# A mixture-of-experts and attention kernel whose scatters add into rows of x in DRAM

## What is computed

```python
x = x + 0.5 * ffn(layernorm(x), router, gate_up, gate_up_bias, down, down_bias)
x = x + attention(layernorm(x), Wq, bq, Wk, bk, Wv, bv, Wo, bo)
x = x + 0.5 * ffn(layernorm(x), ...)      # the same weights again
```

## Time and profile before

| | us |
|---|---|
| time, median of 3 runs | 704.48 (702.71 to 705.45) |
| the profiled execution: span, from first to last instruction | 799.3 |
| what lies around the span in the profiled execution | not shown |
| mean granted TensorE clock, as a share of full speed | 0.913 |

### The profile page before, as it was taken

How to read it: one execution, slowest core, us unless ns; L and a number is a source line. 1 busy time by engine, 2 the same in 40 slices (tenths; PEclk the granted TensorE clock), 3 DMA queues, 4 the chain that set the end, 5 groups by cost and what they waited for, 6 DMA issues and landing times.

```text
span 799.3 us, 13210 instructions
## 1 busy us (share of the span) xinstructions
PE 631.0 (79%) x3712; PEld 527.1 (66%) x3713; DVE 446.0 (56%) x1116; ACT 314.2 (39%) x696; POOL 353.5 (44%) x379
## 2 busy tenths in 40 slices
PE   2673898888878879969998996679898898888900
PEld 2452777776757668858887994568777786767700
DVE  6868653444434436277775986845353444445446
ACT  2663243434333335346663443334243334333400
POOL 2781646565656553513331000155656565656400
PEclk9985999999999998999999999599988999999955
DMA  9871232222222221245542431132212222222179
GB/s 307 295 229 28 73 99 81 70 78 69 85 72 78 78 73 52 93 135 157 157 142 94 150 116 66 8 87 67 79 62 85 70 82 69 79 72 79 54 261 369
DMA packets 52601, 87.99 MB, mean 110 GB/s; under 512 B 16228, under 2 KB 32019, under 8 KB 52054
## 3 DMA queue, kind: packets, MB, share of 16 engines
q1 hardware_dynamic: 17568, 39.52, 15.0%
q0 software_dynamic: 13664, 35.42, 14.3%
q10 hardware_dynamic: 21334, 12.61, 5.1%
HBM read 53.94 MB, written 35.39 MB: 112 GB/s over the span
## 4 chain that ended last, share of the span: by engine, by line
PE 61%; DVE 13%; another core or an unknown queue 8%; DMA 7%; issue 5%; ACT 4%; POOL 0%; SPq 0%; ACTq 0%; DVEq 0%; POOLq 0%
PE ps L854 15%; PE ps L852 13%; PE ps L853 12%; PE ps L843 9%; PE ps L1070 3%; DMA work<-y_dram 3%; PE ps L847 3%; DVE aT_lo L1447 2%; PE ps L877 2%; ACT aT_hi L689 2%; DVE xs L1503 1%; DMA raw_c<-L_ffn_down_proj 1%; PE ps L926 1%; PE ps L869 1%
## 5 line engine op out<-in xcount | busy, mean ns | idle before, releaser
L521 POOL DMA_INDIRECT y_dram<-work,sidx x142 | 142.7, 1005 | 166.7 <-ACT work L706 128.7
L513 POOL DMA_INDIRECT work<-xn_dram,gidx x142 | 140.2, 988 | 47.2 <-issue 43.6
L1455 DVE TENSOR_SCALAR work<-ps 128x256 f32<-128x256 f32 x142 | 57.1, 418 | 147.3 <-issue 83.3
L843 PE MATMUL ps<-cst,work 128*128 128x128 f32 x688 | 109.4, 284 | 29.9 <-DVE aT_lo L1447 22.5
L852 PE MATMUL ps<-up_hi,xT_hi 128*128 x284 | 120.9, 426 | 13.5 <-issue 11.2
L854 PE MATMUL ps<-up_hi,xT_lo 128*128 x284 | 114.1, 402 | 8.6 <-issue 8.2
L853 PE MATMUL ps<-up_lo,xT_hi 128*128 x284 | 113.8, 401 | 8.5 <-issue 7.8
L696 ACT ACTIVATE work<-ps 128x256 f32<-128x256 f32 x142 | 52.1, 393 | 171.7 <-PE ps L854 129.8
L843 PEld LDWEIGHTS ps<-cst,work 128*128 128x128 f32 x688 | 84.3, 145 | 52.3 <-issue 35.3
L852 PE MATMUL ps<-dn_hi,aT_hi 128*128 x284 | 96.7, 340 | 0.0
L706 ACT ACTIVATE work<-ps,slot_gate 128x256 f32<-128x256 f32 x142 | 59.5, 471 | 72.2 <-PE ps L854 54.7
(11 more groups left out here) (172 smaller groups left out, 1136.5 us busy)
## 6 DMA issues: line engine op xcount, KB each, us to landing
work<-y_dram SPq DMA_DIRECT2D x32, 512.0 KB, 4.3
xn_dram<-work ACTq DMA_DIRECT2D x29, 255.0 KB, 2.6
xs<-L_attn_x SPq DMA_DIRECT2D x4, 1024.0 KB, 10.5
work<-q_dram SPq DMA_DIRECT2D x16, 256.0 KB, 2.8
out<-xs SPq DMA_DIRECT2D x16, 256.0 KB, 5.9
q_dram<-work ACTq DMA_DIRECT2D x15, 256.0 KB, 2.3
work<-xn_dram,gidx POOLq DMA_INDIRECT x142
y_dram<-work,sidx POOLq DMA_INDIRECT x142
```

The costliest lines, as they stand in the source:

```text
L513: pool.indirect_dma_start(xg[:, k, u, 1:H + 1], None, xn_dram[n], bass.IndirectOffsetOnAxis(ap=gidx[:, 2 * s + u:2 * s + u + 1], axis=0)). ...
L521: pool.indirect_dma_start(y_dram[n], bass.IndirectOffsetOnAxis(ap=sidx[:, 2 * s + u:2 * s + u + 1], axis=0), ysb[:, k, u, :], None, bounds ...
L843: ins = nc.tensor.transpose(ps[:, bank, k:k + P], src[:, u, c * P:(c + 1) * P], ident)
L1455: return v.tensor_scalar(upv[:, u, :], ps[:, 2 + 2 * b + u, :].rearrange("p (f c) -> p f c", c=2)[:, :, 1], 1.0 - LIMIT, 1.0 + LIMIT, ALU. ...
```

## The change

- `y_dram` goes. In its place stands `sums_dram`, one row for each token and 128 spare ones. In layer 0 SP copies x into it, DRAM to DRAM, in four parts, behind the expert weights. In layer 1 SP stores each pair of xs to it once attention has been added (`x_done`).
- A scatter now adds its 128 rows to the rows of their tokens (`compute_op=ALU.add`). The two choices of a token come in different tiles. Each scatter waits until the one before it has landed; the first of a layer waits for the copy or the stores. The index `sidx` is the token's, or 4096 plus the partition for a slot without a token, and the bounds check is gone (three more VectorE operations in `route`, and SKIP's place).
- In GpSimd's step, gathers and scatters alternate: gather, scatter, gather, scatter.
- After layer 0 SP loads the sums straight into xs, 256 KB a pair, four in flight, each waiting only for the load four before it; `ybuf` and `combine` go.
- The end of layer 1 is four copies, DRAM to DRAM, of 1 MB each, from the sums to the output; the loads, additions and stores there go.

```diff
-        y_dram = [scratch(f"y_dram{n}", [T * TOPK, H]) for n in range(2)]
+        sums_dram = [scratch(f"sums_dram{n}", [T + P, H]) for n in range(2)]
...
+        def part(rows, q):
+
+            n = T // OUT_PARTS
+            return rows[q * n:(q + 1) * n, :].rearrange("(p i) h -> p (i h)", p=P)
...
             for e in range(2, E):
                 load_raw(e)
+            for q in range(OUT_PARTS):
+                sp.dma_start(part(sums_dram[0], q), part(x_rows, q)).then_inc(L[0].sums_begun, 16)
...
             wait_scattered(0)
-            for b in range(2):
-                sp.dma_start(ybuf[:, b], pair(y_v[0], b)).then_inc(L[0].y_loaded[b], 16)
+            for j in range(4):
+                sp.dma_start(pair(xs, j), pair(sums_v[0], j)).then_inc(L[0].sums_loaded[j], 16)
...
-            with sp.Fori(0, NG // 2 - 1) as it:
-                for b in range(2):
-                    g = it * 2 + b
-                    sp.wait_ge(L[0].y_used, g + 1)
-                    sp.dma_start(ybuf[:, b], pair(y_v[0], g + 2)).then_inc(L[0].y_loaded[b], 16)
-
-
-            sp.wait_ge(L[0].y_used, NG)
+            with sp.Fori(0, NG // 4 - 1) as it:
+                for j in range(4):
+                    sp.wait_ge(L[0].sums_loaded[j], 16 * (it + 1))
+                    sp.dma_start(pair(xs, it * 4 + (j + 4)), pair(sums_v[0], it * 4 + (j + 4))
+                                 ).then_inc(L[0].sums_loaded[j], 16)
...
+            with sp.Fori(0, NG) as g:
+                sp.wait_ge(x_done, g + 1)
+                sp.dma_start(pair(sums_v[1], g), pair(xs, g)).then_inc(L[1].sums_begun, 16)
+
             wait_scattered(1)
-            for j in range(4):
-                sp.dma_start(ybuf[:, j], pair(y_v[1], j)).then_inc(L[1].y_loaded[j], 16)
...
-            for j in range(4):
-                finish(NG - 4 + j, j, False)
-            sp.wait_ge(out_stored, 16 * NG)
+            for q in range(OUT_PARTS):
+                sp.dma_start(part(out_rows, q), part(sums_dram[1], q)).then_inc(out_stored, 16)
+            sp.wait_ge(out_stored, 16 * OUT_PARTS)
...
-                def scatter(s):
-                    k = s % RING
-                    for u in range(halves(s)):
-                        pool.wait_ge(l.y_sb, evicted(s, u))
-                        pool.indirect_dma_start(y_dram[n],
-                                                bass.IndirectOffsetOnAxis(ap=sidx[:, 2 * s + u:2 * s + u + 1], axis=0),
-                                                ysb[:, k, u, :], None, bounds_check=T * TOPK - 1,
-                                                oob_is_err=False).then_inc(l.scattered[k], 16)
+                def scatter(s, u):
+                    k = s % RING
+                    rows = bass.IndirectOffsetOnAxis(ap=sidx[:, 2 * s + u:2 * s + u + 1], axis=0)
+                    pool.wait_ge(l.y_sb, evicted(s, u))
+                    if s == 0 and u == 0:
+                        pool.wait_ge(l.sums_begun, 16 * (NG if n else OUT_PARTS))
+                    elif u == 0:
+                        pool.wait_ge(l.scattered[(s - 1) % RING], 32 * ((s - 1) // RING + 1))
+                    else:
+                        pool.wait_ge(l.scattered[k], 32 * (s // RING) + 16)
+                    pool.indirect_dma_start(sums_dram[n], rows, ysb[:, k, u, :], None, compute_op=ALU.add
+                                            ).then_inc(l.scattered[k], 16)
...
                 for s in range(NP):
                     if s + RING < NP:
                         pool.wait_ge(l.x_lo, turned(s))
-                        gather(s + RING)
-                    if s >= 2:
-                        scatter(s - 2)
+                    for u in range(2):
+                        if s + RING < NP and u < halves(s + RING):
+                            gather(s + RING, u)
+                        if s >= 2:
+                            scatter(s - 2, u)
                 for s in range(NP - 2, NP):
-                    scatter(s)
+                    for u in range(halves(s)):
+                        scatter(s, u)
...
+                spare = small[:, 6:7]
+                st.done(v.tensor_scalar(spare, cst[:, C_P:C_P + 1], 0.5, float(T), ALU.mult, ALU.add))
+                st.done(v.tensor_scalar(nam[:, 0, :], nam[:, 1, :], 0.0, spare, ALU.is_equal, ALU.mult))
+                st.done(v.tensor_tensor(sidx[:, :], gidx[:, :], nam[:, 0, :], ALU.add))
...
+                turn()
                 if not (static and g == NG - 1):
-                    combine(L[0], g + 1, 1 - b, it * 2 + (j + 1) // 2, turn)
-                else:
-                    turn()
-                if not (static and g == NG - 1):
-                    dve.wait_ge(L[0].y_used, g + 2)
+                    dve.wait_ge(L[0].sums_loaded[(j + 1) % 4], 16 * (it + 1 + (j + 1) // 4))
                     moments(A, g + 1, 1 - b)
```

More of the change, by code:

```diff
@@ L39 @@
 SKIP = 16384.0
+OUT_PARTS = 4
 WEIGHTS_AT = {2: 0, 4: 1, 6: 2, 8: 3, 10: 4, 12: 5}
@@ L246, in build @@
         aTb = [[t[:, :, :, :] for t in pair] for pair in (aT, aT2)]
-        ybuf = area(0, 4, 2, TOPK, H)
         xn_a = area(2048, 4, 2, H)
@@ L327, in __init__ @@
                 self.y_ps, self.y_sb = s("y_ps"), s("y_sb")
-                self.y_loaded = [s(f"y_loaded_{j}") for j in range(4 if n else 2)]
-                self.y_used = s("y_used")
+                self.sums_begun = s("sums_begun")
+                self.sums_loaded = [s(f"sums_loaded_{j}") for j in range(0 if n else 4)]
         L = [Layer(0), Layer(1)]
@@ L342, in build @@
         x_v = x.rearrange("b (p i) h -> p (b i) h", p=P)
-        out_v = out.rearrange("b (p i) h -> p (b i) h", p=P)
+        x_rows, out_rows = [t.rearrange("b t h -> (b t) h") for t in (x, out)]
         xn_v = [d.rearrange("(p i) h -> p i h", p=P) for d in xn_dram]
-        y_v = [d.rearrange("(p i k) h -> p i k h", p=P, k=TOPK) for d in y_dram]
+        sums_v = [d[0:T, :].rearrange("(p i) h -> p i h", p=P) for d in sums_dram]
         def pair(v, g):
             return v[:, bass.ds(g * 2, 2)]
+        def part(rows, q):
+            n = T // OUT_PARTS
+            return rows[q * n:(q + 1) * n, :].rearrange("(p i) h -> p (i h)", p=P)
         def y_bank(s):
@@ L443, in _ @@
                     sp.dma_start(qin[:, j], pair(q_dram, g + 4)).then_inc(q_loaded[j], 16)
+            with sp.Fori(0, NG) as g:
+                sp.wait_ge(x_done, g + 1)
+                sp.dma_start(pair(sums_v[1], g), pair(xs, g)).then_inc(L[1].sums_begun, 16)
             wait_scattered(1)
-            for j in range(4):
-                sp.dma_start(ybuf[:, j], pair(y_v[1], j)).then_inc(L[1].y_loaded[j], 16)
[L450 to L456, removed]
-                for j in range(4):
-                    finish(it * 4 + j, j, True)
-            for j in range(4):
-                finish(NG - 4 + j, j, False)
-            sp.wait_ge(out_stored, 16 * NG)
+            for q in range(OUT_PARTS):
+                sp.dma_start(part(out_rows, q), part(sums_dram[1], q)).then_inc(out_stored, 16)
+            sp.wait_ge(out_stored, 16 * OUT_PARTS)
         @block.gpsimd
@@ L508, in experts, with gather @@
                 pool.wait_ge(l.routed, 1)
-                def gather(s):
+                def gather(s, u):
                     k = s % RING
-                    for u in range(halves(s)):
-                        pool.indirect_dma_start(xg[:, k, u, 1:H + 1], None, xn_dram[n],
-                                                bass.IndirectOffsetOnAxis(ap=gidx[:, 2 * s + u:2 * s + u + 1], axis=0)
-                                                ).then_inc(first_tile_in if s == 0 and u == 0 else l.gathered[k], 16)
-                def scatter(s):
-                    k = s % RING
-                    for u in range(halves(s)):
-                        pool.wait_ge(l.y_sb, evicted(s, u))
-                        pool.indirect_dma_start(y_dram[n],
-                                                bass.IndirectOffsetOnAxis(ap=sidx[:, 2 * s + u:2 * s + u + 1], axis=0),
-                                                ysb[:, k, u, :], None, bounds_check=T * TOPK - 1,
-                                                oob_is_err=False).then_inc(l.scattered[k], 16)
-                for s in range(RING):
-                    gather(s)
+                    pool.indirect_dma_start(xg[:, k, u, 1:H + 1], None, xn_dram[n],
+                                            bass.IndirectOffsetOnAxis(ap=gidx[:, 2 * s + u:2 * s + u + 1], axis=0)
+                                            ).then_inc(first_tile_in if s == 0 and u == 0 else l.gathered[k], 16)
+                def scatter(s, u):
[10 more added lines that the diff above has]
+                                            ).then_inc(l.scattered[k], 16)
+                for s in range(RING):
+                    for u in range(halves(s)):
+                        gather(s, u)
                 for s in range(NP):
@@ L1496, in experts @@
                 a_lo(NP - 1, 1)
```

(12 more changed lines are left out.)

## The result

The changed kernel takes 985.67 us (983.52 to 990.23, 4 runs) against 704.14 us before: a ratio of 1.4002, 95% interval 1.3959 to 1.4044. It is slower, as forecast, but 281.5 us slower where 134 were forecast, and outside the range of 745 to 945. The profiled execution has a span of 987.4 us.

What follows compares the result with a forecast made beforehand. TensorE and nearly full GpSimd bound the expert stretches; the change makes scatters a waiting chain. Sum: 704.5 + 149.6 (chain) - 15 (tail) - 2.5 (between layers) + 1.6 (small additions) = 838.2 us, range 745 to 945.

Steps and rivals of the forecast that it cites:

- S: Interval between chained scatters on GpSimd's queue: 2.3 to landing, 0.8 to next start, 0.5 for the addition, 3.6 us.
- the addition d: Extra time of a scatter that adds, in each interval of the chain: taken as 0.5 us, bounds 0 to 2.1.
- the gather's row: Nearest traced DMA that reads DRAM: data end 2.4 us after its start, some 0.35 later than a scatter's.
- rival 3: Dear addition in the scatter chain: engines read, add and write in turn, interval 4.3 to 5.2 us, 936 to 1062; chance 0.16.
- the gaps: Stops of TensorE and GpSimd in every second expert step, GpSimd idle 3.5 us; 85 us assumed absent from timed runs.
- The estimate of the stretches: Both expert stretches before the change, in a timed run: 360 of the profile's 445.2 us, 180 a layer.
- The tail: End of layer 1: 35.8 us of loads, additions and stores replaced by four copies taking 21 us, -15.
- Between the layers: After layer 0's last landing: a first load of half the size with no addition behind it, -2.5 us.
- the start: Small additions ahead of layer 0's expert work: three VectorE operations +0.6, store of the gates +1, together +1.6 us.
- A hidden wait (1): Wait ahead of each scatter costs nothing up to an interval of 2.63 us; 689 us in all; chance 0.06.
- a cheap addition (2): Addition near 0 and landing near 2.1 in the scatter chain: interval 2.85 to 3.1 us, 733 to 768; chance 0.12.
- TensorE's clock (4): In the expert stretches the clock falls to 0.58, a step takes 9.1 us, total 967; chance 0.12 of adding over 20.

## Why the prediction was wrong

**The mechanism** was the forecast one: a chain of 71 scatters a layer on GpSimd's queue, all engines at its pace, the gather hidden under the wait. The landing of a plain scatter and the restart (2.3 + 0.8 = 3.1) measured 3.20 in the kernel with the wait alone (2.4 + 0.8). S came out at 4.62 us, not 3.6.

**The step that failed** is the third part of S, the addition d, taken as 0.5 "near the gather's row". It measured 1.42 us (4.62 less 3.20), inside the bounds of 0 to 2.1. Two things were mis-sized. GpSimd's time for an adding scatter, which I left at 1.0 and named only as a thing that would make the prediction wrong, rose to 1.58: 0.59 of the 1.42. And the engines' part was taken as 0.5, from data that end 0.35 us later (the gather's row) and 0.5 us of moving the old row, which together make 0.85. It measured 0.83, nearly their sum. The nearest row misled: a gather's 128 KB goes in 32 packets of 4 KB as a plain scatter's does, while an adding scatter's goes row by row, eight an engine. That is the condition that rival 3 names (S 4.3 to 5.2); it had a chance of 0.16, and the range left most of it out. With S = 4.62 the same sum gives 838 + 140 x 1.02 = 981 us, 5 us from the result. That it comes so near is in part luck: the mean interval is 4.68 us and the last landing 3.7, so the two stretches are 10 us longer than the sum has them, and more than was forecast is given back elsewhere.

**The range** ended at 945, S = 4.36, though the bound of d reached S = 5.2. With one term that no row priced and that counts 140 times, the range should have followed the bounds of that term.

**The rule that was weighed.** By the Trainium skill (Collectives: The Full Stack, "The bandwidth ceiling") the add needs two source reads and is free in itself, which gave an estimate of d = 0.3. The runs show 1.42, 0.83 of it behind GpSimd: that price is too low here, and it has no term for the 0.59 on GpSimd. The Trainium skill's other figure (DMA: Bandwidth & Descriptors, "Anatomy of one DMA"), about 2.0 us and the bytes, 2.3 us by estimate, fits the plain scatter: 3.20 less the restart of 0.8 is 2.4.

**The profile against the times.** I took the gaps for something of the profiled execution. That is not so: timed runs of the kernel before take 800 to 810 us on the chips of the experiments, and the span of every run there lies only 1.8 to 3.0 us below its time. The difference lies between one set of executions and the other, most likely between chips. That is also why the span after lies near the timed median (987.4 and 985.7), a forecast that held for another reason than the one given.

That bears on the comparison of the two profiles. On one of the chips where the kernel before takes 800 us, the changed kernel starts its scatters at 111.4 us (not 108.5), has 207.0 us between the layers (not 201.1) and a tail of 15.3. Beside the profile before (110.4, 207.9, 35.8), which has the length of such a chip, it gives back 20 us outside the stretches and not 29.0. The estimate of the stretches held nevertheless: with 281.5 us measured, 662.3 in the stretches after and 20 to 29 given back, the stretches before take 352 to 361 us on the chip of the result, where I had put 360.

**The rest of the sum.** The tail: 15.5 us, where I took 21 of bounds from 15 to 36. It is the lower of the two sums there, 4.19 MB at the 352 GB/s of loads and stores and 3 us for issue and landing; a byte that is both read and written in DRAM did not cost double. Between the layers -2.5 was forecast and the start +1.6. The two profiles show -6.8 and -1.9; with the changed kernel of the slower chip it is -1.0 and +1.1. So the larger gains may be the chip's and not the change's, and the starts of kernels with the same work up to there lie between 106.6 and 111.4 us. In the stage between, the first load takes 2.78 us instead of 3.94 and its additions are gone, 2.6 us together, as forecast.

The first load after layer 0 in the changed kernel's chain, to set beside the earlier trace rows:

```profile
436.50 3.63 DMA sums_dram<-work,sidx
440.14 0.02 issue
440.15 0.03 SPq L421
440.18 0.04 issue
440.22 2.78 DMA xs<-sums_dram
```

**The rivals.** A hidden wait (1) and a cheap addition (2) are excluded by 3.20 and 4.62. TensorE's clock (4) did fall, to a granted 0.84 and 0.83 in the stretches between its levels of 1.2 and 2.4 GHz, where the kernel before has 0.96 and 0.93, with TensorE busy 67% and 64%. It did not set the pace: TensorE waited 154.9 us for gathers.

## What to carry to other kernels

When an operation that used to stream is put in a chain, its latency counts once per link. Price every part of it, the instruction's own time on the issuing engine included, before looking at what it saves: here 20 to 29 us were saved outside the expert stretches and some 300 to 310 lost in them. If an operation with no row in any trace stands in such a chain, measure it by itself first, or let the range reach to its bounds. And look whether a kernel at full pace has gaps that a slower one lacks: 0.8 us more a step gained 4 to 6% on the chips where it did.

## What was not expected of the hardware

- An indirect DMA that adds keeps GpSimd busy for 1.58 us, a plain one 1.0, with the same 128 rows; for 64 rows it is 1.47 and 0.91.
- Behind that an adding scatter of 128 rows of 1 KB takes 0.83 us longer than a plain one, and one of 64 such rows 0.35. It moves each row in a packet of its own, 128 of 1 KB at 0.145 us where a plain one has 32 of 4 KB at 0.18.
- A scatter that waits for the one before starts 0.8 us after that one's landing; where the queue runs ahead, GpSimd stands still for 0.30 us between two.
- A DRAM to DRAM copy of 4.19 MB in four parts, issue and landing included, took 15.5 us.
- The same kernel takes 704 us on one chip and 800 to 810 on four others. There TensorE's work is interrupted in about every second step of the expert stretches (in the profile before 25 of 56 steps take over 7 us), and the gaps mostly vanish when a step is stretched from 5.2 to 6.0 us: 0.944, 0.961 and 0.951 of the time. What makes the gaps was not settled; the granted clock stays at 1.00 in the one from 207 to 212 us.
